# One-core recommender kernel: own-result waits between W1's low parts, a group of gathers moved to the copied table, and new orders for the first two tiles

## The chip, the cores and the metric

The kernel runs on one core of one Trainium2 chip. The metric is the device time of one execution in microseconds (us); three runs of the kernel before took 774.78, 777.32 and 778.52, the median is 777.32.

The core's engines run programs of their own and meet in semaphores: TensorE (PE) multiplies and transposes, VectorE (DVE) and ScalarE (ACT) do elementwise steps, GpSimd (POOL) issues the gathers, SyncE (SP) the plain DMAs.

## The reference

A batch of 2048 rows is scored. Each row has 13 continuous values and 26 categories. Every category picks a row of 64 numbers in a table of 12500 rows; every continuous value scales one of the table's first 13 rows. The 39 vectors, their 741 pairwise dot products and two dense layers with layer norm give one number a row:

```python
cont_emb = emb_table[:CONT_FIELD][None, :, :] * conts[:, :, None]
cate_emb = emb_table[cates]
cc = jnp.concatenate([cont_emb, cate_emb], axis=1)
gram = jnp.einsum('bfd,bgd->bfg', cc, cc)
pairs = gram[:, ROWS, COLS]
X = jnp.concatenate([cont_emb.reshape(B, -1), cate_emb.reshape(B, -1), pairs], axis=1)
X = jax.nn.relu(_layernorm(X @ W1 + b1, ln1_g, ln1_b))     # W1: 3237 x 1024
X = jax.nn.relu(_layernorm(X @ W2 + b2, ln2_g, ln2_b))     # W2: 1024 x 1024
logit = jax.nn.sigmoid(X @ Wout + bout)
```

Categories may lie past the table's end; such an index means the last row.

## The kernel before

**Tiles.** The batch is cut into 16 tiles of 128 rows. For a tile, the 26 fields' rows are gathered into `xb`, one gather of 128 rows for each field, in four groups: fields 0-7, 8-13, 14-19, 20-25 (`GROUPS` counts pairs of fields). TensorE transposes a group (L570, "own 1" to "own 3" and "next 0"), then 19 k-tiles of 128 rows of W1 are multiplied into the sums: 0 to 12 are gathered rows, 13 to 18 are features (pairs, continuous values). Between them stand the gram products (L612), whose results ScalarE and VectorE take out of PSUM (`take_dots`), turn into features and hand back to TensorE for transposing ("factor", "late").

**Split numbers.** Every operand is used as a rounded high part and the rest, its low part, so a k-tile is six matmuls (high times high, high times low, low times high, in two halves of 512 columns; L546 to L548). For W1 this is done once: ScalarE rounds part k (`w1_hi_part`, L855), VectorE subtracts that from the raw part (`w1_lo_part`, L1129, a tensor_tensor of 128x1024 with both inputs in SBUF). For each transposed group ScalarE rounds (`split_group`, L787), VectorE subtracts (L1115), and both make copies for the gram products (`gram_copies`, L794 and L800; `still_low`, L1123).

**Order.** Nothing is scheduled by a program at run time: each engine runs its list in the order written. TensorE's order in a tile is a tuple: `FIRST` for tile 0, `SECOND` for tile 1, `STEADY` for the others. A number is a k-tile (13 and up belong to the tile before, except at the end), "own g" a group's transposes, "v n" products of the continuous rows of W1. ScalarE and VectorE have their counterparts in `first_tile`, `second_tile` and `iteration`.

**Gathers.** GpSimd (`gather`, L494) issues 26 gathers a tile in the order of the fields, from L510 or L513. There is one `xb`, so a group's gathers of tile x+1 wait until that group of tile x is transposed (`trans_ready`). In the loop further waits (`progress`) tie them loosely to TensorE's other steps. The table lies in DRAM as it came; indices past its end can't be gathered from it, so tile 0's gathers check bounds and skip such rows (L510), and ScalarE has filled `xb` with the last row before (`fill`, L867). Meanwhile SyncE copies the table into a scratch table with 128 copies of the last row behind it (four copies, `table_in`, and `last_rows_in`); the index of an absent row is set to one of these (`limit`), and from tile 1 on the gathers need no check (L513). The copies stand in SyncE's list of loads behind W1's part 6; each load waits until the one four places ahead has landed (L438).

**Start.** VectorE first makes tile 0's indices (`index_chain`), then the others, then the constants of the gram products, then `cont_features(0)`, and then W1's low parts 0 to 3.

## Time and profile before

| | |
|---|---|
| median of 3 runs | 777.32 us |
| the profiled execution | 778.39 us, its span 776.9 us |
| mean granted TensorE clock | 0.979 of full |
| busy: PE, DVE, ACT, POOL | 731.6, 582.2, 516.1, 481.3 us |
| gathers from the copied table | 390, 978 ns each |

The span is what the trace covers; about 1.5 us of the time lie outside it. Busy time leaves out the issue of DMAs and waits on semaphores. In a timeline a row gives the start, the duration, the engine, the line, what is written from what, and in brackets how long the engine idled before and what it waited for; "x4" merges four instructions in a row. "<-issue" is a gap in which the engine waited for nothing that the profile shows; between two gathers of GpSimd it is 0.30 us. A landing is the time from a DMA's issue to its end; for a gather the issue is the start of its row.

### The profile page before, as it was taken

Reading aid. Unit: us, or ns where it says so; the run is one execution under the profiler, and the core shown is the slowest. Engines: PE = TensorE matmul, PEld = TensorE weight load, DVE = VectorE, ACT = ScalarE, POOL = GpSimd, SP = SyncE. Lnnn points to the kernel's source line nnn. Section 1 sums busy time; section 2 is a strip of 40 time slices with the busy share of each in tenths; the row PEclk is TensorE's granted clock in tenths of the full one; section 3 lists DMA queues with packets and bytes.
Section 4 is the critical chain, followed back from the end, with each engine's and each line's share of the span. In section 5 each row is a group of like instructions: output and inputs, shape, how many; then the busy total and the mean of one; then the engine's idle time right before and its main releaser. Section 6 shows DMA issues by size and latency. Waiting matters only on the chain.

```text
span 776.9 us, 11960 instructions
## 1 busy us (share of the span) xinstructions
PE 731.6 (94%) x3583; PEld 596.8 (77%) x3583; DVE 582.2 (75%) x1735; ACT 516.1 (66%) x978; POOL 481.3 (62%) x450
## 2 busy tenths in 40 slices
PE   5598899999999999999999999999999999999995
PEld 1356778888888888778788877878878888888884
DVE  7357977878878888787787877878787566565568
ACT  3487877868778687686867868677665535545441
POOL 6777877777777777777777777777000433434431
PEclk9798979999999999999999999999999999999998
DMA  8961111111111111111111111112463111101000
GB/s 323 347 228 25 23 54 28 54 54 26 54 39 40 52 25 52 34 45 52 25 54 25 52 54 26 52 25 59 176 216 124 55 29 54 54 27 54 27 1 0
DMA packets 26644, 53.37 MB, mean 69 GB/s; under 512 B 11024, under 2 KB 11351, under 8 KB 26554
## 3 DMA queue, kind: packets, MB, share of 16 engines
q1 hardware_dynamic: 10570, 31.29, 12.0%
q0 software_dynamic: 13312, 13.06, 7.3%
q10 hardware_dynamic: 2736, 8.71, 2.8%
q8 instruction: 12, 0.20, 0.1%
q14 instruction: 14, 0.11, 0.1%
HBM read 45.20 MB, written 11.63 MB: 73 GB/s over the span
## 4 chain that ended last, share of the span: by engine, by line
PE 44%; POOL 30%; issue 17%; DVE 4%; DMA 2%; ACT 2%; POOLq 0%; ACTq 0%; DVEq 0%
POOL xb L513 27%; PE acc L546 13%; PE acc L548 13%; PE acc L547 13%; POOL xb L510 3%; PE gr L612 1%; PE tr L612 1%; DMA xb<-in_L_rec_emb_table,idx_all 1%; PE gr L714 1%; PE tr L714 1%; DMA xb<-table_scratch,idx_all 1%; PE tr L570 0%; PE gr L570 0%; DMA last_row<-in_L_rec_emb_table 0%; ACT dots L830 0%
## 5 line engine op out<-in xcount | busy, mean ns | idle before, releaser
L513 POOL DMA_INDIRECT xb<-table_scratch,idx_all x390 | 381.3, 978 | 118.9 <-issue 116.4
L546 PE MATMUL acc<-w_hi,x_hl 128*128 128x512 f32 x416 | 172.9, 416 | 4.5 <-DVE x_hl L1115 3.1
L548 PE MATMUL acc<-w_hi,x_hl 128*128 128x512 f32 x416 | 165.5, 398 | 0.0
L547 PE MATMUL acc<-w_lo,x_hl 128*128 128x512 f32 x416 | 165.0, 397 | 0.0
L530 POOL TENSOR_TENSOR raw_lo<-raw_lo,raw_hi 128x1024 f32<-128x1024 f32 x14 | 33.5, 2391 | 146.8 <-ACT raw_lo L998 146.8
L546 PE MATMUL acc<-w_hi 128*128 128x512 f32 x256 | 100.9, 394 | 0.0
L548 PE MATMUL acc<-w_hi,w_lo 128*128 128x512 f32 x256 | 99.7, 389 | 0.0
L547 PE MATMUL acc<-w_lo,w_hi 128*128 128x512 f32 x256 | 99.7, 389 | 0.0
L794 ACT CAST g_still<-x_hl 64x384 fp32r<-64x384 f32 (+1 forms) x128 | 97.9, 765 | 2.5
L546 PEld LDWEIGHTS acc<-w_hi,x_hl 128*128 128x128 f32 x416 | 80.0, 192 | 20.8 <-issue 4.1
L548 PEld LDWEIGHTS acc<-w_hi,x_hl 128*128 128x128 f32 x416 | 79.7, 192 | 18.5
L547 PEld LDWEIGHTS acc<-w_lo,x_hl 128*128 128x128 f32 x416 | 80.2, 193 | 13.3
L546 PE MATMUL acc<-w_hi,f_slots 128*128 128x512 f32 x192 | 77.9, 406 | 1.5 <-DVE w_lo L1129 1.5
L548 PE MATMUL acc<-w_hi,f_slots 128*128 128x512 f32 x192 | 75.0, 391 | 0.0
L547 PE MATMUL acc<-w_lo,f_slots 128*128 128x512 f32 x192 | 75.0, 390 | 0.0
L1369 DVE TENSOR_TENSOR w_lo<-raw_lo,w_hi 128x256 fp32r<-128x256 f32 x64 | 34.9, 564 | 50.4 <-ACT w_hi L990 50.3
L800 ACT ACTIVATE g_move<-x_hl 64x384 fp32r<-64x384 f32 (+1 forms) x128 | 70.3, 549 | 1.5
L800 ACT CAST g_move<-x_hl 64x384 fp32r<-64x384 f32 (+1 forms) x128 | 69.0, 539 | 1.9
L836 ACT ACTIVATE st<-st 128x1 f32<-128x1 f32 x32 | 6.5, 203 | 77.6 <-DVE st L1219 77.6
L548 PEld LDWEIGHTS acc<-w_hi,w_lo 128*128 128x128 f32 x256 | 48.1, 188 | 10.0
L547 PEld LDWEIGHTS acc<-w_lo,w_hi 128*128 128x128 f32 x256 | 48.1, 188 | 9.4
L546 PEld LDWEIGHTS acc<-w_hi 128*128 128x128 f32 x256 | 48.1, 188 | 9.5
(121 smaller groups left out, 1313.3 us busy)
## 6 DMA issues: line engine op xcount, KB each, us to landing
raw_lo<-in_L_rec_W SPq DMA_DIRECT2D x26, 512.0 KB, 5.4
h_scratch<-h_row ACTq DMA_DIRECT2D x16, 512.0 KB, 2.9
raw_hi<-h_scratch SPq DMA_DIRECT2D x16, 512.0 KB, 3.5
xb<-table_scratch,idx_all POOLq DMA_INDIRECT x390, 2.4
table_scratch<-in_L_rec_emb_table SPq DMA_DIRECT2D x4, 781.2 KB, 7.9
raw_hi<-in_L_rec_W SPq DMA_DIRECT2D x6, 512.0 KB, 5.7
raw_hi<-in_L_rec_b SPq DMA_DIRECT2D x1, 512.0 KB, 4.3
raw_hi<-in_L_rec_ln_g SPq DMA_DIRECT2D x1, 512.0 KB, 5.2
```

The costliest lines, as they stand in the source:

```text
L510: done = nc.gpsimd.indirect_dma_start(out=to, out_offset=None, in_=emb, in_offset=at_row, bounds_check=VOCAB - 1, oob_is_err=False)
L513: done = nc.gpsimd.indirect_dma_start(out=to, out_offset=None, in_=table, in_offset=at_row)
L530: nc.gpsimd.tensor_tensor(a2[par][:, :], n2[par][:, :], g2_bc, ALU.mult).then_inc(a2_mul, 1)
L546: nc.tensor.matmul(o, a, w, start=first, stop=False)
L547: nc.tensor.matmul(o, a, v, start=False, stop=False)
L548: return nc.tensor.matmul(o, b, w, start=False, stop=last)
L612: last = nc.tensor.matmul(to, g_still[:, SAMPLES * j:SAMPLES * (j + 1), :].rearrange("p s f -> p (s f)"), g_move[:, :, j:P:P // SAMPLES], ...
L714: last = nc.tensor.transpose(t[:, k // 4, (k % 4) * P:(k % 4 + 1) * P], h1[par][:, k * P:(k + 1) * P], ident[:, :])
L794: nc.scalar.copy(still_to(0, a, b, of), still_from(a, b, of))
L800: last = nc.scalar.mul(to, x_hi, 2.0) if m % 2 else nc.scalar.copy(to, x_hi)
L836: nc.scalar.activation(st[:, 1:2], st[:, 0:1], ACT.Sqrt).then_inc(sqrt_done, 1)
L1369: TT(y_lo[:, par, part, :], y[:, part, :], y_hi[:, par, part, :].bitcast(F32), ALU.subtract).then_inc(y_split, 1)
```

## The change

It has five parts.

1. `w1_lo_part(k)` waits, for k of 1 and more, until part k-1 is reported done (`w1_split`), so VectorE waits for its own result.
2. Tile 0's fourth group (fields 20 to 25) is gathered from the copied table without a check. The waits for the four copies and the last rows move from behind tile 0's gathers to ahead of these six, with one for all indices; that group isn't filled, and the first index chain makes 20 columns instead of 26.
3. SyncE issues the first load of `e13` ahead of `last_row`.
4. W1's parts stand elsewhere. Before: 0-3, 4, 5-6, 7, 8, 9-10, 11, 12, then 13 to 18 one by one. After, on VectorE: 0-5, 6, 7-8, 9-12, 13-14, 15-16, 17-18, and `cont_features(0)` behind part 6. ScalarE rounds in the same groups up to 12, and 13 to 18 in one go as before.
5. In tiles 0 and 1 the order is new: in `FIRST` the v products stand one place earlier each, in `SECOND` "late prev" comes after k-tiles 13, 14 and 4; `copy_v` goes ahead of the first `take_dots`; in tile 1 `take_dots(1, 0)` goes into `norm1(0)`, behind the root.

```diff
-FIRST = (0, 1, 2, 3, "own 1", 4, 5, 6, "own 2", "v 3", 7, 8, "v 4", "own 3", "v 5", 9, 10, "gram 0", "gram 1", 11,
+FIRST = (0, 1, 2, 3, "own 1", 4, 5, 6, "v 3", "own 2", "v 4", 7, 8, "v 5", "own 3", 9, 10, "gram 0", "gram 1", 11,
          "gram 2", "gram 3", "next 0", 12)
-SECOND = (0, 1, 2, 3, "factor prev", "own 1", "late prev", 13, 4, 14, 5, 15, 6, "own 2", 16, 17, 18, 7, "own 3", 8, 9,
+SECOND = (0, 1, 2, 3, "factor prev", "own 1", 13, 14, 4, "late prev", 15, 5, 6, "own 2", 16, 17, 18, 7, "own 3", 8, 9,
           "gram 0", "gram 1", 10, "gram 2", "gram 3", 11, "next 0", 12)
...
+            sp.dma_start(e13[:, 0, :], emb[0:CONT, :]).then_inc(e13_in, 16)
             sp.dma_start(last_row[:, :], emb[VOCAB - 1:VOCAB, :].to_broadcast([P, DIM])).then_inc(last_row_in, 16)
-            sp.dma_start(e13[:, 0, :], emb[0:CONT, :]).then_inc(e13_in, 16)
...
                 for g, (a, b) in enumerate(GROUPS):
-                    if first:
+                    bounded = first and g < NG - 1
+                    if bounded:
                         pool.wait_ge(filled, g + 1)
+                    elif first:
+                        pool.wait_ge(idx_done, 2)
+                        table_whole()
...
-            for g in range(NG):
+            for g in range(NG - 1):
                 fill(g)
-            w1_hi_parts(0, 1, 2, 3)
+            w1_hi_parts(0, 1, 2, 3, 4, 5)
             split_group(0, 0)
-            w1_hi_part(4)
+            w1_hi_part(6)
             act.wait_ge(setup_done, 1)
             gram_copies(0, 0)
-            w1_hi_parts(5, 6)
             split_group(0, 1)
             gram_copies(0, 1)
-            w1_hi_part(7)
+            w1_hi_parts(7, 8)
...
                 split_group(0, 2)
-                w1_hi_part(8)
                 gram_copies(0, 2)
-                w1_hi_parts(9, 10)
+                w1_hi_parts(9, 10, 11, 12)
                 split_group(0, 3)
                 gram_copies(0, 3)
-                w1_hi_part(11)
+                copy_v()
                 for q in range(FILLS):
                     take_dots(0, q, first=True)
-                w1_hi_part(12)
-                copy_v()
...
                 dve.wait_ge(w1_rounded, k + 1)
+                if k >= 1:
+                    dve.wait_ge(w1_split, k)
                 TT(w1_lo[:, k, :], raw_lo[k][:, :], w1_hi[:, k, :].bitcast(F32),
                    ALU.subtract).then_inc(w1_split, 1)
...
+            w1_lo_parts(0, 1, 2, 3, 4, 5)
+            split_group(0, 0)
+            w1_lo_part(6)
+            still_low(0, 0)
             cont_features(0, first=True)
-            w1_lo_parts(0, 1, 2, 3)
-            split_group(0, 0)
-            w1_lo_part(4)
-            still_low(0, 0)
-            w1_lo_parts(5, 6)
             split_group(0, 1)
             still_low(0, 1)
-            w1_lo_part(7)
+            w1_lo_parts(7, 8)
```

## Rows read from the trace of the kernel before

**Rows 1.** The page: chain that ended last, shares of span by line.

```profile
POOL xb L513 27%; PE acc L546 13%; PE acc L548 13%; PE acc L547 13%; POOL xb L510 3%; PE gr L612 1%; PE tr L612 1%; DMA xb<-in_L_rec_emb_table,idx_all 1%; PE gr L714 1%; PE tr L714 1%; DMA xb<-table_scratch,idx_all 1%; PE tr L570 0%; PE gr L570 0%; DMA last_row<-in_L_rec_emb_table 0%; ACT dots L830 0%
```

**Rows 2.** TensorE's waits, total, times, longest; 110-300 us, then 300-580.

```profile
PE acc L546 <- DVE x_hl L1115: 0.3, 1, 0.3
...
PE gr L570 <- DMA xb<-table_scratch,idx_all: 7.1, 8, 1.1
```

**Rows 3.** Transposes of group 0, tiles 2 and 3; GpSimd's timeline, 117 us.

```profile
L570 PE MATMUL tr<-ident,xb x4: 290/404/421, 109.3 to 109.9; 128*128 128x128 f32 x4
...
L570 PE MATMUL tr<-ident,xb x4: 270/272/273, 141.3 to 141.7; 128*128 128x128 f32 x4
...
117.69 0.94 POOL L513 DMA_INDIRECT xb<-table_scratch,idx_all  x1 [0.30 <-issue]
```

**Rows 4.** GpSimd's groups in three stretches: busy, mean ns | idle before.

```profile
L510 POOL DMA_INDIRECT xb<-in_L_rec_emb_table,idx_all x26 | 32.2, 1239 | 12.4 <-issue 7.6 <-ACT xb L867 4.8
...
L513 POOL DMA_INDIRECT xb<-table_scratch,idx_all x32 | 36.4, 1138 | 9.8 <-issue 9.4 <-PE tr L570 0.3
...
L513 POOL DMA_INDIRECT xb<-table_scratch,idx_all x359 | 345.9, 963 | 109.4 <-issue 107.3 <-PE tr L570 0.9 <-PE tr L612 0.6
```

**Rows 5.** TensorE's timeline: start us, us, instruction, [idle before].

```profile
549.37 0.55 PE L570 MATMUL gr<-ident,xb 128*128 128x128 f32 x3 [0.78 <-DMA xb<-table_scratch,idx_all]
```

**Rows 6.** GpSimd's timeline: gathers of tiles 0 and 1.

```profile
6.24 1.34 POOL L510 DMA_INDIRECT xb<-in_L_rec_emb_table,idx_all  x1 [4.75 <-ACT xb L867]
...
14.39 1.00 POOL L510 DMA_INDIRECT xb<-in_L_rec_emb_table,idx_all  x1 [0.30 <-issue]
15.69 5.53 POOL L510 DMA_INDIRECT xb<-in_L_rec_emb_table,idx_all  x1 [0.30 <-issue]
...
37.48 1.54 POOL L510 DMA_INDIRECT xb<-in_L_rec_emb_table,idx_all  x1 [0.30 <-issue]
...
51.20 1.55 POOL L513 DMA_INDIRECT xb<-table_scratch,idx_all  x1 [0.30 <-issue]
53.06 0.94 POOL L513 DMA_INDIRECT xb<-table_scratch,idx_all  x1 [0.30 <-issue]
```

**Rows 7.** VectorE's timeline: setup's end, low parts 0-3, parts 9-10.

```profile
12.86 0.70 DVE L1108 MEMSET g_still<- 64x768 f32 x1 [0.20 <-issue]
...
15.73 4.63 DVE L1129 TENSOR_TENSOR w_lo<-raw_lo,w_hi 128x1024 fp32r<-128x1024 f32 x4
...
50.71 2.36 DVE L1129 TENSOR_TENSOR w_lo<-raw_lo,w_hi 128x1024 fp32r<-128x1024 f32 x2 [1.92 <-ACT w_hi L855]
```

**Rows 8.** VectorE's timeline: the second step waits for the first.

```profile
5.57 0.36 DVE L1054 TENSOR_SCALAR spare<-spare 128x390 f32<-128x390 f32 x1
5.96 0.57 DVE L1056 TENSOR_TENSOR spare<-spare 128x390 f32<-128x390 f32 x1
```

**Rows 9.** ScalarE's timeline: W1's third rounded half.

```profile
14.97 1.04 ACT L855 CAST w_hi<-raw_lo 128x1024 fp32r<-128x1024 f32 x1 [0.38 <-DMA raw_lo<-in_L_rec_W]
```

**Rows 10.** SyncE's timeline: the load that waits for the last table copy.

```profile
30.07 0.33 SPq L438 DMA_DIRECT2D raw_hi<-in_L_rec_W  x1
```

**Rows 11.** DMA issues at 14.39, 15.69, 46.36 us: issue to landing.

```profile
xb<-in_L_rec_emb_table,idx_all POOLq DMA_INDIRECT x1, 6.0
...
xb<-in_L_rec_emb_table,idx_all POOLq DMA_INDIRECT x1, 12.7
...
xb<-table_scratch,idx_all POOLq DMA_INDIRECT x1, 5.9
```

**Rows 12.** TensorE's timeline: three starts after a wait.

```profile
28.49 1.09 PE L570 MATMUL tr<-ident,xb 128*128 128x128 f32 x4 [7.32 <-DMA xb<-in_L_rec_emb_table,idx_all]
...
66.69 0.79 PE L546 MATMUL acc<-w_hi,x_hl 128*128 128x512 f32 x1 [1.36 <-DVE w_lo L1129]
...
79.11 0.50 PE L546 MATMUL acc<-w_hi,f_slots 128*128 128x512 f32 x1 [1.54 <-DVE w_lo L1129]
```

**Rows 13.** Busy PE, PEld, DVE, ACT, POOL; granted clock, DMA share, GB/s.

```profile
97.00:110.00 13.00, 11.41 (x49) 9.62 (x49) 9.78 (x24) 8.60 (x17) 9.68 (x11) 0.61 0.21 66
```

More of the change, by code:

```diff
@@ L492, in progress, with table_whole @@
                     stands_alone(pool)
+            def table_whole():
+                for n in range(COPIES):
+                    pool.wait_ge(table_in[n], 16)
+                pool.wait_ge(last_rows_in, 16)
             def gather(x, par, first=False, tied=False):
@@ L508, in gather @@
                         at_row = bass.IndirectOffsetOnAxis(ap=idx[:, par, f:f + 1], axis=0)
-                        if first:
+                        if bounded:
                             done = nc.gpsimd.indirect_dma_start(out=to, out_offset=None, in_=emb, in_offset=at_row,
@@ L516, in _ @@
             gather(0, 0, first=True)
-            for n in range(COPIES):
-                pool.wait_ge(table_in[n], 16)
-            pool.wait_ge(last_rows_in, 16)
             gather(1, 1)
@@ L918, in first_tile @@
                 split_group(1, 1)
+                still_copies(1, 0)
+                move_copies(1, 0, (0, 1))
                 late_features_hi(0)
-                still_copies(1, 0)
+                move_copies(1, 0, (2, 3))
                 tail_features_hi(0)
-                move_copies(1, 0)
             def second_tile():
@@ L930, in second_tile @@
                 gram_copies(1, 3)
-                norm1(0, 0)
+                root(0)
+                take_dots(1, 0)
+                norm1(0, 0, rooted=True)
                 h1_store(0)
-                for q in range(FILLS):
+                for q in range(1, FILLS):
                     take_dots(1, q)
@@ L1058, in index_chain @@
                 TS(to.bitcast(I32), f, 0.0, most, ALU.max, ALU.min).then_inc(count, 1)
-            index_chain(0, 0, CATE, idx[:, 0, :], float(VOCAB), idx_done)
+            bounded = 2 * GROUPS[NG - 1][0]
+            index_chain(0, 0, bounded, idx[:, 0, 0:bounded], float(VOCAB), idx_done)
             dve.wait_ge(rows_in, 16)
             nc.vector.tensor_copy(limit[:, :], rows_sb[:, :]).then_inc(idx_step, 1)
-            index_chain(4, CATE, TILES * CATE, idx_all[:, CATE:TILES * CATE], limit[:, 0:1])
+            index_chain(4, bounded, TILES * CATE, idx_all[:, bounded:TILES * CATE], limit[:, 0:1])
             dve.wait_ge(idx_step, 8)
@@ L1285, in first_tile @@
                 split_group(0, 2)
-                w1_lo_part(8)
                 still_low(0, 2)
-                w1_lo_parts(9, 10)
+                w1_lo_parts(9, 10, 11, 12)
                 split_group(0, 3)
@@ L1291, in first_tile @@
                 indices(2, 0)
-                w1_lo_part(11)
                 for q in range(FILLS):
                     take_dots(0, q, first=True)
-                w1_lo_part(12)
                 split_group(1, 0)
@@ L1298, in first_tile @@
                 cate_features(0)
+                w1_lo_parts(13, 14)
+                factor_lo(0)
+                split_group(1, 1)
                 cate_pairs(0)
-                factor_lo(0)
-                w1_lo_part(13)
-                split_group(1, 1)
+                w1_lo_parts(15, 16)
                 late_features_lo(0)
-                w1_lo_part(14)
                 tail_features_lo(0)
-                w1_lo_part(15)
                 still_low(1, 0)
-                w1_lo_part(16)
             def second_tile():
+                w1_lo_parts(17, 18)
+                split_group(1, 2)
                 still_low(1, 1)
-                w1_lo_part(17)
-                split_group(1, 2)
-                w1_lo_part(18)
                 still_low(1, 2)
@@ L1320, in second_tile @@
                 indices(3, 1)
-                norm1(0, 0)
-                for q in range(FILLS):
+                norm1(0, 0, lambda: take_dots(1, 0))
+                for q in range(1, FILLS):
                     take_dots(1, q)
```

## The prediction

> **What bounds the kernel now.** I read the chain that ended last first [rows 1]: the largest single entry is GpSimd issuing the gathers of the tile loop, 27% of the span in busy time and most of the 17% "issue" beside it, and no TensorE line has more than 13%. So although TensorE is busy 94% of the span, the end of the tile loop hangs on another engine. The waits of TensorE show when [rows 2]: between 110 and 300 us it waits 0.3 us in all, between 300 and 580 us it waits 7.1 us in eight pieces, each for the rows that a gather brings. The pace explains it. TensorE starts tile 2 at 109.3 and tile 3 at 141.3, 32.0 us a tile [rows 3]. GpSimd makes 359 gathers from 92 us to the last in 345.9 + 109.4 us [rows 4], which is 1.268 us each and 26 x 1.268 = 33.0 us a tile. TensorE begins late, gains about 1 us a tile on GpSimd, catches up at about 300 us and from there goes at GpSimd's pace. The last gathered group is transposed at 549.37 after a wait of 0.78 us for its DMA [rows 5], and the rest follows from it. Hence the rule for this change: **the end moves by what GpSimd's last gather moves**, as long as TensorE's work on the first tiles doesn't fall back by more than those 7.1 us against it.
>
> GpSimd in turn never waits in the loop for TensorE: every gap between gathers is its usual 0.30. When tile 3's first gather starts at 117.69, the transposes that free its buffer are long done (they start at 109.3) [rows 3]; the margin is some 7.6 us. So what matters on GpSimd is how long each gather takes. Undisturbed, one takes 1.00 us against the input table and 0.94 against the copied one [rows 6]. In tile 0 the 26 take 1239 ns on average, from 46 to 92 us 32 take 1138 ns, and after that 963 [rows 4]. The excess is 26 x 0.24 = 6.2 and 32 x 0.194 = 6.2, together **12.4 us**, all of it in the time in which VectorE makes W1's low parts.
>
> Rows 6 and 7 together show what holds GpSimd. The gather at 15.69 takes 5.53 us and ends at 21.22; VectorE's four low parts run back to back from 15.73 to 20.36, and the gather ends 0.86 after them. The gather at 51.20 ends at 52.75; a low part runs from 50.71 to 51.93, and again it ends 0.82 later, in the middle of the next low part. So a gather needs something 0.13 us into its run that a low part holds for its 1.22 us; having got it, it needs 0.82 to 0.87 more. In the second case the following part had only just got its rounded half from ScalarE, and the gather came in between; in the first all were ready ahead, and it didn't until all four were over. All but two of the longer gathers up to 92 us end like this behind a low part (the two are the first, 0.34 us too long [rows 6], and one with some 0.15), so of the 12.4 us about 11.9 belong to the 19 low parts: 4.5 to the first four and 7.4 to the other fifteen, 0.49 each.
>
> **The change, part by part.**
>
> *The wait between low parts.* VectorE may begin part k only when part k-1 is reported done. Steps that wait for their own engine's result follow at 0.04 us behind the end (5.57 + 0.36, then 5.96) [rows 8], where unhindered parts overlap by 0.08 (four take 4.63, not 4.88) [rows 7]: 0.12 us for each part that follows another directly, 12 of them, 1.4 us of VectorE spread over 75 us. In the first train the loads set the pace anyway (next edit), so the idle time covers it there; it isn't covered ahead of split_group(0, 3), which waits behind parts 9 to 12 (four waits, 0.5 us; below). What it brings: between two parts what the gather needs is free for about 0.04 us, so a waiting gather should hold out one part at most. After it got in, it asks again 1.30 us later (0.87 + 0.30 + 0.13; 1.25 against the copied table), and the parts recur every 1.26: they nearly keep step, so a train of parts costs one wait at its start, not one for each part. The pair at 50.71 behaves so already: the first part holds a gather for 0.61, the second none (53.06 takes 0.94) [rows 6, 7]. What the trace can't show is a train of four or six ready parts with the wait; its bounds are 0 and the full back-to-back time.
>
> *The order of the low parts.* Now they come as 0-5, 6, 7-8, 9-12, 13-14, 15-16, 17-18: seven trains. Taking cont_features(0) from ahead of part 0 lets VectorE begin at 13.6 instead of 15.73 [rows 7]. The parts then come at the pace of the loads, 1.4 us (a rounded half takes 1.04 and waits 0.38 for its DMA) [rows 9], with gaps of 0.15 to 0.2, so the first train is loose. I take 0.55 for each of the seven (near the 0.49 of the isolated ones), and 0.8 more for what gets out of step inside the trains of six and four: 7 x 0.55 + 0.8 = 4.6, plus the 0.5 of the two others, 5.1. Gain on GpSimd 12.4 - 5.1 = **7.3 us**; bounds 2.4 (every part still costs 0.5) and about 10 (nothing but the looseness is left), and below nothing if the gap doesn't let the gather in (a rival below).
>
> [...]
>
> *Group 3 of tile 0 from the copied table.* Six gathers at 1.25 instead of 1.30 apart: 0.3 us gained. The new waits stand ahead of them on GpSimd, where the whole loop's gathers queue behind. The copies' last piece has landed when SP issues the load at 30.07, which waits for it [rows 10]. Before, the group's first gather starts at 37.48 [rows 6]; it comes at about 34 to 35 now. So 4 us of cover, and each us beyond would cost one us at the end. These gathers now bring whole rows, 32 KB each, while W1 still loads; the first such gather in that traffic lands 5.9 us after its issue, 2.0 of them its making, no later than those from the input [rows 11]. Their indices now come from the second chain of steps, whose third step begins at 5.96 [rows 8]. The last fill disappears from ScalarE (0.5 us, off every path).
>
> *The first rows swapped on SP.* last_row lands some 0.45 us later, and the first fill with it; the first gather waits for its indices too, and starts 0.9 after those. I charge 0.2 us, bounds 0 and 0.45.
>
> *TensorE, VectorE and ScalarE in tiles 0 and 1.* Here only TensorE's place relative to GpSimd is at stake. Group 0 lands at 28.4, 12.7 us after the issue of its last gather, where the one before took 6.0 [rows 11]; with the gather ending at 17 to 18 it lands at 22 to 24, and TensorE's 7.32 us wait [rows 12] shrinks by 5. A little is lost at split_group(0, 3), behind parts 9 to 12 (it ends at about 51 now, at 53.7 before). Part 12's wait for its low half (66.69, 1.36 us) goes, of that at 79.11 (1.54) half, since parts 13 to 16 stand earlier; and gram 2 of tile 1 no longer sits behind all of norm1 on ScalarE; before, the granted clock there is 0.61 over 13 us [rows 13], part of them at the lower of the two levels. "late prev" moves back by three k-tiles, some 4 us; the gather of tile 2's field 10 waits for it, but is due only after 36 gathers from 46 us on, past 90 us, where "late prev" comes near 75. Together TensorE comes into tile 2 by 8 to 11 us earlier, so more than GpSimd. It then catches GpSimd some three tiles sooner, and there two things follow: its waits grow from 7.1 to about 10 us, and GpSimd goes in locked step with the loop, where gathers lose 0.6 us a tile to short VectorE steps instead of the 0.15 to 0.3 of the free tiles (average 0.47: 0.018 x 26). I charge 1.0 for that, bounds 0 and 1.5.
>
> **The sum:** 7.3 + 0.3 - 0.2 - 1.0 = 6.4 us. The profiled run took 778.39 (span 776.9), 1.1 over the median of the runs; 778.4 - 6.4 = 772.0 for a like run and 777.3 - 6.4 = 770.9 for the median. I say **771**.
>
> **The rivals.**
> (a) *Every low part still costs its 0.5 us*, trains or not, because gathers and parts don't fall into step. Then 19 x 0.5 + 0.5 = 10 us of excess stay, gain 2.4 + 0.3 - 0.2 = 2.5: 774.8. For it: the trains of one and two have shown nothing longer. Against it: the pair at 50.71.
> (b) *The wait opens nothing* (slower). A gap of 0.04 us is too short, and the gather that asks at a train's start comes in at its end. Then the train 0-5 holds from 14.5 to about 22.3, 7.8 us, 9-12 4.4, four pairs 1.8 each (7-8, 13-14, 15-16, 17-18), part 6 0.55: 20 us against 12.4, so 8 slower with the small terms: 785. It decides once the holds exceed 12.4, that is when more than about ten parts pass in closed trains. For it: the 5.53 at 15.69. Against it: no part there waited for anything, and in the pair the gather got in without any gap.
> (c) *The trains cost nothing* and TensorE's head start isn't spent: gain about 10, 767.
> [...]
>
> **How the numbers follow.** The forecast 0.66 (its own range 767.5 to 774), (a) 0.15, (b) 0.08, (c) 0.08, (d) 0.03. The range 766 to 777 takes in the forecast, (a) and most of (c). A measurement of this kernel can tell about 0.5% from no change, 3.9 us: faster is below 773.4. Faster: most of the forecast and (c), 0.70; same: (a), (d) and the forecast's upper edge, 0.23; slower: 0.07.
>
> **What would show it.** No gather over about 2.3 us; mean gather of tile 0 near 1.10 us instead of 1.24, and near 1.03 from there to the last low part; last gather starting near 539 instead of 545.3; TensorE waiting for gathered rows from about 200 us on, in more pieces; tile 2 starting near 100. It would be wrong if the gather of field 20 starts late behind the table, if a gather still spans several low parts, or if TensorE's waits in the loop vanish, since then TensorE and not GpSimd sets the end.

## The result and the profile after

| | before | after |
|---|---|---|
| median of 11 runs | 777.32 us (774.13 to 778.52) | 770.82 us (769.32 to 774.43) |
| the profiled execution, its span | 778.39, 776.9 | 770.79, 769.3 |
| ratio of the runs | | 0.9928, 95% interval 0.9911 to 0.9945 |

The changed kernel is faster by 0.7%, 6.5 us in the medians, 5.6 us by the ratio and 7.6 us between the two profiled executions. The forecast was 771, from a gain of 6.4 us.

The line of the page that answers to [rows 1], the chain that ended last, still has the gathers of the loop first (L513 has become L523, the transposes' L570 L577, the low parts' L1129 L1138):

```profile
POOL xb L523 26%; PE acc L553 14%; PE acc L554 13%; PE acc L555 13%; PE gr L619 1%; PE tr L619 1%; PE gr L721 1%; PE tr L721 1%; DMA xb<-in_L_rec_emb_table,idx_all 1%; PE tr L577 1%; ACT g_move L807 1%; DMA h_scratch<-h_row 1%; DVE w_lo L1138 1%; DVE g_still L1130 1%; DVE dots L1204 1%
```

GpSimd's timeline of the changed kernel: the stretch of the 5.53 us gather of [rows 6], the first gather from the copied table, the longest gather of the kernel, and the last:

```profile
13.01 1.00 POOL L520 DMA_INDIRECT xb<-in_L_rec_emb_table,idx_all  x1 [0.30 <-issue]
14.31 1.29 POOL L520 DMA_INDIRECT xb<-in_L_rec_emb_table,idx_all  x1 [0.30 <-issue]
15.91 1.02 POOL L520 DMA_INDIRECT xb<-in_L_rec_emb_table,idx_all  x1 [0.30 <-issue]
17.24 1.02 POOL L520 DMA_INDIRECT xb<-in_L_rec_emb_table,idx_all  x1 [0.31 <-issue]
...
33.91 0.96 POOL L523 DMA_INDIRECT xb<-table_scratch,idx_all  x1 [0.30 <-issue]
...
37.68 1.99 POOL L523 DMA_INDIRECT xb<-table_scratch,idx_all  x1 [0.30 <-issue]
...
538.12 0.95 POOL L523 DMA_INDIRECT xb<-table_scratch,idx_all  x1 [0.30 <-issue]
```

VectorE's timeline beside it: the first six low parts and the four of the later train.

```profile
13.51 7.87 DVE L1138 TENSOR_TENSOR w_lo<-raw_lo,w_hi 128x1024 fp32r<-128x1024 f32 x6
...
45.49 5.21 DVE L1138 TENSOR_TENSOR w_lo<-raw_lo,w_hi 128x1024 fp32r<-128x1024 f32 x4 [2.71 <-ACT w_hi L862]
```

The first low part (13.51 to 14.73) holds the gather at 14.31 until its end, which costs 0.29; from then on the gathers come between the parts and lose 0.02 each. The last gather starts at 538.12, where it started at 545.31 before: 7.2 us earlier. The groups of GpSimd's gathers up to 60 us answer to [rows 4] (mean ns of one):

```profile
L520 POOL DMA_INDIRECT xb<-in_L_rec_emb_table,idx_all x20 | 21.5, 1075 | 10.6 <-issue 5.5 <-ACT xb L874 4.8 <-DMA table_scratch<-in_L_rec_emb_table 0.3
L523 POOL DMA_INDIRECT xb<-table_scratch,idx_all x20 | 20.6, 1028 | 6.1 <-issue 6.1
```

Below, "excess" is the sum over a kernel's gathers of what each takes beyond 1.00 us (input table) or 0.945 us (copied table), added up from the timeline. Up to 92 us it is 12.4 us before and 5.0 after; from 92 us on 6.1 and 6.3. A gather "asks" about 0.12 us into it: the 0.94 that an undisturbed one takes less the 0.82 that it still takes once let in (0.13 of the 1.00 against the input table, with 0.87); what it does at that point isn't shown. Of the 5.0 us the first parts of the seven trains hold back gathers by 0.29, 0.95, 1.05, 0.29, 0, 0.94 and 0.52 us, 0.58 on average.

TensorE's waits from 300 to 580 us answer to [rows 2], its first transposes of tile 2 to [rows 3]:

```profile
PE gr L577 <- DMA xb<-table_scratch,idx_all: 6.6, 8, 1.0
...
L577 PE MATMUL tr<-ident,xb x4: 272/272/273, 101.1 to 101.4; 128*128 128x128 f32 x4
```

Tile 2 starts at 101.1 instead of 109.3. TensorE's granted clock at tile 1's end, 0.61 in [rows 13] (0.50 in every us from 100 to 109, 1.00 in the three before 99 and from 110 to 111), is 0.88 in the 10 us up to its end now, and 0.95 in the next 10 us (busy time by stretch: PE, PEld, DVE, ACT, POOL, granted clock, DMA share, GB/s):

```profile
90.00:100.00 10.00, 7.16 (x42) 6.45 (x43) 8.55 (x22) 7.97 (x16) 7.56 (x9) 0.88 0.24 79
100.00:110.00 10.00, 9.55 (x45) 7.36 (x43) 9.60 (x42) 8.42 (x13) 7.87 (x8) 0.95 0.11 28
```

One table carries much of what follows (e8_after is the changed kernel profiled once more). It is read from the timelines: excess up to 92 us and behind it, start of tile 2 on TensorE, length of a tile in the early and the late loop, last gather, start of the last gathered group's transposes, and the time of the same execution.

| kernel | excess to 92, after | tile 2 | a tile, early and late | last gather | last transposes | time |
|---|---|---|---|---|---|---|
| before | 12.4, 6.1 | 109.3 | 32.0, 33.1 | 545.3 | 549.4 | 778.4 |
| after | 5.0, 6.3 | 101.1 | 32.0, 33.1 | 538.1 | 541.7 | 770.8 |
| e1_before_wait | 8.6, 4.5 | 104.9 | 32.0, 33.1 | 540.1 | 543.6 | 772.7 |
| e2_after_nowait | 6.9, 6.1 | 101.9 | 32.0, 33.1 | 539.8 | 543.2 | 772.2 |
| e3_after_notable | 4.1, 5.4 | 101.9 | 32.0, 33.1 | 536.4 | 540.0 | 769.0 |
| e4_before_cont | 5.8, 7.0 | 102.5 | 32.0, 33.1 | 539.8 | 543.3 | 775.1 |
| e5_tensor_more | 5.6, 5.9 | 102.4 | 32.0, 33.1 | 537.7 | 541.2 | 770.2 |
| e6_gpsimd_more | 6.1, 6.6 | 100.3 | 32.8, 33.1 | 543.8 | 547.4 | 776.4 |
| e8_after | 6.7, 7.2 | 102.4 | 32.0, 33.2 | 540.3 | 543.8 | 774.8 |
| e9_halves | 4.9, 5.9 | 107.1 | 32.0, 32.7 | 537.4 | 540.9 | 770.8 |
| e11_pairs4 | 6.3, 0.0 | 104.6 | 32.4, 32.4 | 532.8 | 541.2 | 770.9 |
| e12_pairs2 | 4.6, -0.6 | 103.1 | 33.2, 33.2 | 534.1 | 551.3 | 781.3 |

### The profile page after: what moved, and what is told of

Its sections match the earlier page's. It is cut to its first block, busy times and chain, and to the rows that moved or that the text cites. A ratio compares the mean times of both kernels' runs of the same rounds, so it can differ in the third digit from the quotient of the medians.

```text
span 769.3 us, 11972 instructions
## 1 busy us (share of the span) xinstructions
PE 727.8 (95%) x3583; PEld 593.4 (77%) x3583; DVE 582.9 (76%) x1735; ACT 515.9 (67%) x977; POOL 474.0 (62%) x450
## 4 chain that ended last, share of the span: by engine, by line
PE 47%; POOL 27%; issue 15%; DVE 6%; DMA 2%; ACT 2%; POOLq 0%; SPq 0%; ACTq 0%; DVEq 0%
POOL xb L523 26%; PE acc L553 14%; PE acc L554 13%; PE acc L555 13%; PE gr L619 1%; PE tr L619 1%; PE gr L721 1%; PE tr L721 1%; DMA xb<-in_L_rec_emb_table,idx_all 1%; PE tr L577 1%; ACT g_move L807 1%; DMA h_scratch<-h_row 1%; DVE w_lo L1138 1%; DVE g_still L1130 1%; DVE dots L1204 1%
## 5 line engine op out<-in xcount | busy, mean ns | idle before, releaser
L523 POOL DMA_INDIRECT xb<-table_scratch,idx_all x396 | 384.8, 972 | 120.7 <-issue 120.1
```

The source lines that it names most:

```text
L523: done = nc.gpsimd.indirect_dma_start(out=to, out_offset=None, in_=table, in_offset=at_row)
```

## The experiments

### Is the wait worth something by itself?

e1_before_wait: the kernel before with the wait alone.

```diff
                 dve.wait_ge(w1_rounded, k + 1)
+                if k >= 1:
+                    dve.wait_ge(w1_split, k)
```

> The kernel before with the own-result wait alone. Theory (the wait opens the train): the gather at 15.69 us gets in after the first low part, at 16.95, and ends 0.87 later, so it takes about 2.1 us instead of 5.53; the next ones keep step and lose about 0.1 each. Gain on GpSimd 3.2 us, the median about 774 against 777.3. The other low parts stand alone or in pairs that were already open: nothing more. Rival (the wait opens nothing, a gap that short is too short): the gather still takes 5.5 us or a little more, 777.3. Rival (TensorE sets the end, not GpSimd): the gather gets short but the time stays at 777.3.

Measured: 772.82 us median, ratio 0.9954 (0.9936 to 0.9972). GpSimd's and VectorE's timelines:

```profile
15.69 2.13 POOL L510 DMA_INDIRECT xb<-in_L_rec_emb_table,idx_all  x1 [0.30 <-issue]
```

```profile
15.73 5.20 DVE L1131 TENSOR_TENSOR w_lo<-raw_lo,w_hi 128x1024 fp32r<-128x1024 f32 x4
```

The gather that starts at 15.69 beside the same four parts takes 2.13 instead of 5.53, as the theory had it (2.1), and the time falls by 3.6 us, over half of what the whole change brings (the kernel before, run beside it on the same chip, has a median of 776.37). "The wait opens nothing" has fallen.

e2_after_nowait: the changed kernel with those two lines taken out again.

> The changed kernel without the own-result wait. Theory: the first six parts are paced by the loads (1.4 us apart) and stay open even so, no gather above 1.3 us there; but parts 9 to 12 and the pairs 13-14, 15-16, 17-18 have their rounded halves ready ahead, close up, and hold a gather until the train's end: up to 4.6 us at 46 us and up to 2.3 us at each pair. GpSimd loses some 3.5 us against the changed kernel, 774.3 (range 772.5 to 777). Rival (the order alone did it, the wait gives nothing): 770.8 with the same gathers as in the changed kernel. Rival (b) of the forecast turned round (the waits only cost VectorE its 0.19 us a part): 770 or less.

Measured: 773.61 us median, ratio 0.9977 (0.9958 to 0.9996). So without the wait a third of the gain is left by the ratios, and the wait is worth 2.8 us in the medians, 3.8 by the ratios, on top of the new order. The one profiled execution says less: it took 772.18 us, its excess is 6.9 against 5.0 and its last gather starts 1.6 us later than the changed kernel's; four of the twelve runs took 776.5 to 777.9, and none of those was profiled. Nor do the traces show the loss where I had put it. GpSimd and VectorE around the train 9 to 12, around 13 and 14, and around 15 and 16:

```profile
47.55 1.33 POOL L523 DMA_INDIRECT xb<-table_scratch,idx_all  x1 [0.30 <-issue]
49.18 1.96 POOL L523 DMA_INDIRECT xb<-table_scratch,idx_all  x1 [0.30 <-issue]
...
67.69 0.94 POOL L523 DMA_INDIRECT xb<-table_scratch,idx_all  x1 [0.30 <-issue]
...
74.20 3.01 POOL L523 DMA_INDIRECT xb<-table_scratch,idx_all  x1 [0.30 <-issue]
```

```profile
46.84 4.63 DVE L1136 TENSOR_TENSOR w_lo<-raw_lo,w_hi 128x1024 fp32r<-128x1024 f32 x4 [2.71 <-ACT w_hi L862]
...
66.58 2.37 DVE L1136 TENSOR_TENSOR w_lo<-raw_lo,w_hi 128x1024 fp32r<-128x1024 f32 x2
...
71.71 2.42 DVE L1210 TENSOR_TENSOR dots<-h_row 128x25 f32<-128x25 f32 x25
74.05 2.35 DVE L1136 TENSOR_TENSOR w_lo<-raw_lo,w_hi 128x1024 fp32r<-128x1024 f32 x2
```

The train 9 to 12 runs back to back (4.63 us for four) and lets a gather in twice: the one at 47.55 ends at 48.88, the one at 49.18 at 51.14, each 0.82 behind the end of one part. It is open. The pair at 74.05 isn't: its gather ends at 77.21, 0.81 behind both parts. What differs is what VectorE did before: it idled 2.71 us ahead of the first, and came without a gap from 25 short steps into the second. The four parts of the kernel before [rows 7] came without a gap from cont_features' twelve short steps:

```profile
14.10 1.72 DVE L1144 SCALAR_TENSOR_TENSOR feats<-ee_bc,c 128x12 f32<-128x12 f32 x12
```

The pair at 66.58 came without a gap from seven short steps, and the gather at 67.69, which asked just as its first part ended, wasn't held. Whether seven are too few or the moment was lucky isn't shown. Within the first train, where I expected no gather above 1.3 us, one that starts at 15.97 takes 2.04.

e4_before_cont: the kernel before with cont_features(0) moved and nothing else.

```diff
-            cont_features(0, first=True)
             w1_lo_parts(0, 1, 2, 3)
             split_group(0, 0)
             w1_lo_part(4)
             still_low(0, 0)
+            cont_features(0, first=True)
```

> The kernel before with one move only: cont_features(0) goes from ahead of W1's low parts 0 to 3 to behind still_low(0, 0). No wait is added. Theory: the parts begin at 13.6 us and then follow the rounded halves, 1.4 us apart, so none is ready ahead: the train is open by itself and the 5.53 us gather becomes one of at most 2.2. Gain 4 us on GpSimd, 773.3 - the same as the wait gives, from the other side. Rival (only a reported result opens the train): a gather of 4 us or more remains between 14 and 21 us, 777.

Measured: 773.34 us median, ratio 0.9960 (0.9942 to 0.9978). GpSimd's timeline of e4_before_cont has no gather above 1.9 us:

```profile
14.37 1.86 POOL L510 DMA_INDIRECT xb<-in_L_rec_emb_table,idx_all  x1 [0.30 <-issue]
16.54 1.30 POOL L510 DMA_INDIRECT xb<-in_L_rec_emb_table,idx_all  x1 [0.30 <-issue]
```

So the wait and the move each take the 5.53 us gather away by themselves. Added to the kernel before, they bring 3.6 and 3.0 us in the medians (776.37 beside them on the same chip), 3.6 and 3.1 by the ratios. e4 can't tell why the move helps: its parts no longer follow short steps, but the second and third also wait 0.38 and 0.35 us for their rounded halves, which is what I had expected, and either can be what lets a gather in. Its excess falls by 6.6 us, more than the time does.

### What holds a gather

Two kernels of their own put gathers beside steps of VectorE of one kind at a time.

```python
# e7_port: for each kind, four steps beside eight gathers (five of the eight kinds; waits between the steps left out here)
TT(r[k][:, :], a[:, :], b[:, :], ALU.subtract)             # two inputs in SBUF
TT(r[k][:, :], flat(ps), b[:, :], ALU.subtract)            # one in PSUM
TT(flat(pw), a[:, :], b[:, :], ALU.subtract)               # two in SBUF, result in PSUM
nc.vector.tensor_copy(c[:, :], a[:, :])
nc.vector.tensor_scalar(r[k][:, :], a[:, :], 0.5, None, ALU.mult)
```

> A kernel of its own that computes nothing of the reference; its output is a constant. GpSimd issues 64 gathers of 128 rows back to back, then 24 plain DMAs of 128 rows; during every eight of them VectorE runs one train of four steps of 128x1024 and then idles: (1) tensor_tensor with both inputs in SBUF, (2) the same with an own-result wait, (3) one input in PSUM, (4) copies f32 SBUF to SBUF, (5) both inputs in SBUF and the result in PSUM with own-result waits, (6) tensor_scalar SBUF to SBUF, (7) tensor_tensor with a short copy between, (8) the same in halves of 512; beside the plain DMAs (1), (4) and nothing. [...]

VectorE's timeline of e7_port, and GpSimd's beside it:

```profile
7.75 4.63 DVE L92 TENSOR_TENSOR r<-a,b 128x1024 fp32r<-128x1024 f32 x4 [1.40 <-issue]
...
28.00 4.62 DVE L97 TENSOR_TENSOR r<-ps,b 128x1024 fp32r<-128x1024 f32 x4 [10.20 <-POOLq L55]
...
54.12 5.08 DVE L104 TENSOR_TENSOR pw<-a,b 128x1024 f32<-128x1024 f32 x4 [10.60 <-POOLq L55]
67.05 2.62 DVE L106 TENSOR_SCALAR r<-a 128x1024 fp32r<-128x1024 f32 x4 [7.85 <-POOLq L55]
...
106.59 4.63 DVE L92 TENSOR_TENSOR r<-a,b 128x1024 fp32r<-128x1024 f32 x4 [8.43 <-POOLq L55]
```

```profile
8.72 1.10 POOL L61 DMA_INDIRECT xb<-in_emb,idx  x1 [0.30 <-issue]
10.12 1.94 POOL L61 DMA_INDIRECT xb<-in_emb,idx  x1 [0.30 <-issue]
...
28.92 0.94 POOL L61 DMA_INDIRECT xb<-in_emb,idx  x1 [0.30 <-issue]
30.16 0.95 POOL L61 DMA_INDIRECT xb<-in_emb,idx  x1 [0.30 <-issue]
...
54.24 1.92 POOL L61 DMA_INDIRECT xb<-in_emb,idx  x1 [0.89 <-DMA xb<-in_emb,idx]
...
67.23 1.33 POOL L61 DMA_INDIRECT xb<-in_emb,idx  x1 [0.61 <-DMA xb<-in_emb,idx]
...
108.29 0.53 POOL L63 DMA_DIRECT2D xb<-in_emb  x1 [1.17 <-DMA xb<-in_emb,idx]
110.00 0.53 POOL L63 DMA_DIRECT2D xb<-in_emb  x1 [1.18 <-DMA xb<-in_emb,idx]
```

The trace has 64 gathers, 0.30 us apart beside the first three kinds and up to 1.10 later, and 24 plain DMAs. VectorE idles 0.42 us between the first two trains and 6.29 to 10.63 ahead of each other one. What the gathers that asked during each train took:

| VectorE's steps of 128x1024 | gathers in order, us |
|---|---|
| tensor_tensor, both inputs in SBUF | 1.10, 1.94 |
| the same, own-result waits | 1.22, 0.96, 0.95, 0.95 |
| tensor_tensor, one input in PSUM | 0.94, 0.95, 0.94 |
| copies f32, SBUF to SBUF | 1.33, 0.94 |
| both inputs in SBUF, result in PSUM, own-result waits | 1.92, 0.97, 0.94 |
| tensor_scalar, SBUF to SBUF | 1.33, 1.19 |
| both inputs in SBUF, a short copy between | 1.88, 0.94, 0.94 |
| both inputs in SBUF, in halves of 512 | 1.33, 0.94, 1.01 |

Beside steps with one input in PSUM a gather takes its 0.94 to 0.95. Beside steps with two inputs in SBUF it is held even when their result goes to PSUM (54.24: 1.92, ending 0.82 behind the first step), and also by tensor_scalar and by copies (1.33 each, 0.82 behind a step's end), until the end of the one step that runs; the second gather beside the copies (0.94) asked just as one of them ended (42.89). Plain DMAs issued by GpSimd take 0.53 to 0.55 beside the same tensor_tensor train that holds gathers, and 0.53 beside nothing. So for tensor_tensor what counted is where VectorE reads and not where it writes, and a plain DMA wasn't held by it. Why a gather is held and a plain DMA isn't, the rows don't show. Where an own-result wait or a short copy stands between the steps, one gather takes 1.22 or 1.88 us and the next 0.94 to 0.96.

Copies are another case: beside them plain DMAs take up to 0.84 us, and four in a row end 0.11 to 0.12 us behind the end of a copy each (the first at 118.32, behind 118.20). They are held too, so which side a copy holds isn't separated here, and tensor_scalar wasn't run beside plain DMAs.

But no gather as long as the 5.53 us of [rows 6] came: four ready parts back to back (from 7.75) let a gather in behind the first and behind the third (it ends at 9.82 and 12.06), where the kernel before had them closed. The halves were open too, with 1.33 us at most. The second kernel asks what makes the difference.

> A kernel of its own that computes nothing of the reference; its output is a constant. GpSimd issues gathers of 128 rows back to back. Beside them VectorE runs trains of tensor_tensor steps of 128x1024 with both inputs in SBUF, each kind three times at three offsets of some 0.3 us: (1) four after idling, (2) four directly behind 12 short scalar_tensor_tensor steps with two SBUF inputs, (3) four behind 25 short tensor_tensor steps, (4) four behind 12 short copies, (5) as (2) with an own-result wait before all but the first of the four, (6) eight after idling, (7) four after idling, each with a wait that is met long ahead. Question: in the kernel before four parts held one gather to their end, but four in the last kernel of this sort let one in at every end. [...] Theory B (waits that are met ahead make the difference): (7) closed, (2) to (4) as (1). Theory C (it's the moment at which the gather asks): no kind is always closed, and it depends on the offset alone.

The gathers beside each train of four (each kind three times; "eight" is one train of eight steps):

| VectorE before the four parts | longest gather in the three tries, us |
|---|---|
| 12 short scalar_tensor_tensor steps | 4.78, 5.02, 5.31 |
| 25 short tensor_tensor steps | 5.12, 5.37, 4.39 |
| 12 short copies | 5.22, 5.46, 4.46 |
| 12 short steps, own-result waits between the four | 1.35, 1.61, 1.90 |
| idle (two of three tries ran into each other) | 1.97 |
| idle, eight parts | 1.97, 1.98, 1.97 |
| idle, each part with a wait met long ahead | 1.97, 1.98, 1.96 |

Nine of nine trains behind short steps are closed: the gather ends 0.82 behind the last part. One of them, VectorE and then GpSimd:

```profile
71.76 1.86 DVE L101 SCALAR_TENSOR_TENSOR shorts<-a,b,c 128x12 f32<-128x12 f32 x12 [10.45 <-ACTq L79]
73.54 4.62 DVE L114 TENSOR_TENSOR r<-a,b 128x1024 fp32r<-128x1024 f32 x4
```

```profile
73.67 5.31 POOL L65 DMA_INDIRECT xb<-in_emb,idx  x1 [0.30 <-issue]
```

All the others are open (1.98 us at most). It made no difference whether the short steps were tensor_tensor (4.39 to 5.37), scalar_tensor_tensor (4.78 to 5.31) or copies (4.46 to 5.46), nor whether the parts carry a wait that is met long ahead (1.96 to 1.98; theory B), nor which of the three moments it was (theory C); in all nine the gather asked while the first part ran. With the own-result wait the train behind short steps was open three times of three (1.35 to 1.90). Why a run of short steps closes what follows isn't shown; the rows show only that it did.

The rows of this kernel show a second use of the wait, in GpSimd's timeline beside a train of four with it (from 202.34) and a train of eight without it (from 242.81):

```profile
202.75 1.61 POOL L65 DMA_INDIRECT xb<-in_emb,idx  x1 [0.30 <-issue]
204.67 0.96 POOL L65 DMA_INDIRECT xb<-in_emb,idx  x1 [0.30 <-issue]
205.93 0.95 POOL L65 DMA_INDIRECT xb<-in_emb,idx  x1 [0.31 <-issue]
...
243.71 1.15 POOL L65 DMA_INDIRECT xb<-in_emb,idx  x1 [0.30 <-issue]
245.16 1.97 POOL L65 DMA_INDIRECT xb<-in_emb,idx  x1 [0.30 <-issue]
247.43 1.97 POOL L65 DMA_INDIRECT xb<-in_emb,idx  x1 [0.30 <-issue]
249.70 1.98 POOL L65 DMA_INDIRECT xb<-in_emb,idx  x1 [0.30 <-issue]
```

Without the wait the parts recur every 1.14 us, a gather asks every 1.25, and so it falls just behind the start of a part again and again: 1.02 us lost each time, in every second part. With the wait they recur every 1.26 and the gathers fit between them: one hold at the start, then 0.01 each. So an open train without waits still cost a third of its length (0.21 and three times 1.02 in 9.17 us); one with waits cost one hold (0.67 us here).

### Does GpSimd set the end?

e5_tensor_more gives TensorE work, e6_gpsimd_more gives GpSimd work, both early in the kernel.

```diff
# e5_tensor_more
-                for kt in range(a, b):
+                again = 12 if isinstance(x, int) and x == 2 and g == 2 else 1
+                for kt in [kt for _ in range(again) for kt in range(a, b)]:
# e6_gpsimd_more
             gather(0, 0, first=True)
+            for n in range(26):
+                if n >= 1:
+                    pool.wait_ge(idled, n)
+                nc.gpsimd.memset(small[:, 15:16], 0.0).then_inc(idled, 1)
             gather(1, 1)
```

> The changed kernel; in tile 2 TensorE makes the transposes of group 2 twelve times instead of once, the same values into the same place: 33 transposes of 0.11 us, 3.7 us more of TensorE's work, just past the start. Theory (GpSimd sets the end of the tile loop, TensorE has 7.6 us of waits to give): TensorE's waits for gathered rows shrink from 7.6 to about 4 us and the time stays within 1 us of 770.8. Rival (TensorE sets the end): the time rises by 3.7 us to 774.5 and the waits stay.

> The changed kernel; between tile 0's and tile 1's gathers GpSimd makes 26 small memsets of one unused column, each waiting for the one before. The trace will tell how much that delays the next gather; I estimate 4 us from the 0.45 us pitch of GpSimd's two dependent steps at the start less their size, so anything from 3 to 12. Theory (GpSimd sets the end): the time rises by what the last gather is late, one for one, within 1 us. Rival (TensorE sets the end and GpSimd is ahead): less than half of it arrives.

Measured: 769.74 us for e5 (0.9906, 0.9877 to 0.9936) and 776.27 us for e6 (0.9989, 0.9973 to 1.0004). TensorE's waits from 105 to 580 us, first of e5, then of e6:

```profile
PE gr L578 <- DMA xb<-table_scratch,idx_all: 3.3, 4, 1.0
```

```profile
PE gr L582 <- DMA xb<-table_scratch,idx_all: 12.7, 14, 1.9
```

In e5 tile 2 takes 35.2 us instead of 31.7, TensorE's waits for gathered rows fall from 7.5 (6.6 from 300 us on, 1.0 before; rounded) to 3.3, and the end doesn't move. In e6 the memsets hold tile 1's first gather back by about 4.5 us and the excess is 1.1 higher; the last gather comes 5.7 later, the profiled time is 5.6 longer, and TensorE waits 5.2 us more. One for one, as predicted. The column of last gathers says the same: in all kernels of the table but e4, e8, e11 and e12 the time is 232.4 to 233.4 us behind it. In e4 it is 235.3: there TensorE waits once for VectorE's features behind the last gather, 2.4 us where the changed kernel waits 1.3, and its granted clock in the stretch from 560 to 570 us is 0.83 against 1.00. In e8 it is 234.4, with 3.1 us of that wait. So the end is the last gather's to within some 2 us, which are lost behind it. TensorE's own start counts for little: in e9 it comes into tile 2 at 107.1, 6 us later than in the changed kernel, and the time is the same.

### Can more be had there?

e8_after is the changed kernel again, on the chip of the next one.

> The changed kernel itself, on the same chip as the next one. All theories: 770.8, 0.9928 of the kernel before; GpSimd's excess over undisturbed gathers in the first 90 us again about 5 us, in other places by how the low parts fall.

> The changed kernel with every low part made in two steps of 512 columns, each waiting for the one before. Theory (a gather is held by the one step that runs when it asks for its indices, and gets in at that step's end): a hold costs at most 0.69 us instead of 1.22, the seven trains cost 0.3 each instead of 0.55 on average, and the excess goes from 5.2 to about 3 us; but steps now recur every 0.78 us and no longer keep step with the gathers (1.30), so inside the trains a gather may meet a step each time at a new place: up to 0.3 each. Time 769 to 771. Rival (each such wait costs VectorE 0.19 us and that counts, or the holds are as many as steps): 771 to 773, or excess unchanged.

```diff
-                TT(w1_lo[:, k, :], raw_lo[k][:, :], w1_hi[:, k, :].bitcast(F32),
-                   ALU.subtract).then_inc(w1_split, 1)
+                for h in range(2):
+                    if 2 * k + h:
+                        dve.wait_ge(w1_split, 2 * k + h)
+                    part = slice(h * HALF, (h + 1) * HALF)
+                    TT(w1_lo[:, k, part], raw_lo[k][:, part], w1_hi[:, k, part].bitcast(F32),
+                       ALU.subtract).then_inc(w1_split, 1)
```

Measured: 771.00 for e8 (0.9927, 0.9905 to 0.9949), 770.70 for e9 (0.9922, 0.9901 to 0.9944): the same. In e8's own profiled execution (774.76 us) the excess was 6.7, in e9's (770.76) 4.9: most single holds are shorter (0.2 to 0.3; two take 0.5 and 0.6), but 18 gathers lose over 0.12 us where 8 did, since steps every 0.76 us don't fit a gather. The theory's doubt about the step was right and its 3 us weren't; that a gather asks for its indices at that moment was my guess, and the rows show only that it is held there. e8 against the first profile of the same kernel also tells how much one execution differs from the next: the excess up to 92 us by 1.7 us, the last gather by 2.2, the time by 4.0, of which 1.8 are lost behind the last gather.

e11_pairs4 and e12_pairs2 put own-result waits into the 25 short steps of cate_pairs, in which most later tiles hold a gather for 0.5 us.

```diff
                 for f in range(CATE - 1):
+                    if f and f % 4 == 0:                       # e12: every second
+                        dve.wait_ge(pair_step, 6 * x + f // 4)
                     last = TT(chosen[:, cate_at(f):cate_at(f + 1)], S[:, f, f + 1:CATE], S[:, f + 1:CATE, f], ALU.add)
+                    if (f + 1) % 4 == 0:
+                        last.then_inc(pair_step, 1)
```

> The changed kernel, and VectorE also waits for its own result after every fourth of the 25 short steps that add up a tile's category pairs. In the changed kernel a gather is held about 0.5 us in this run of steps in ten of the fourteen later tiles. Theory (what a gather needs isn't handed over inside a run of short steps, and GpSimd still sets the end): a wait every 0.4 us lets it in, the holds of 0.5 become 0.2 at most, GpSimd saves 2 to 4 us over the loop, VectorE spends 0.6 us more a tile in time it has; 768 (767 to 770). Rival (the hold has another cause, or TensorE takes over as the bound since VectorE is later): excess in the loop stays at 6 us or TensorE waits for VectorE instead; 771 or more.

> The same with a wait after every second step. Theory: the holds there fall to 0.1, but VectorE spends 1.2 us more a tile; 768 if VectorE has that time, otherwise above the kernel with a wait after every fourth, and TensorE's or ScalarE's waits for VectorE show it.

Measured: 770.87 (0.9922, 0.9893 to 0.9952) and 782.55 (1.0075, 1.0047 to 1.0103). The holds of the loop vanish in e11: excess 0.0 instead of 6.3, last gather at 532.77, 5.4 us earlier than in the changed kernel. Nothing of it arrives in the time. TensorE's waits from 105 to 580 us, first of e11, then of e12:

```profile
PE tr L592 <- DVE feats L1178: 1.6, 1, 1.6
PE acc L554 <- DVE x_hl L1123: 1.4, 2, 1.2
```

```profile
PE acc L554 <- DVE x_hl L1123: 13.3, 14, 1.6
```

TensorE no longer waits for a gather at all, and a tile takes 32.4 us from the first to the last, where it took 32.0 while TensorE was free and 33.1 while GpSimd led. The six waits a tile cost TensorE's own loop 0.4 us in each of 13 tiles, some 5 us; with twelve waits a tile takes 33.2, and TensorE waits for VectorE's low half of a group in every tile. The bound changed hands. That e11 comes out even is partly chance: TensorE came into tile 2 at 104.6, 3.5 us later than in the changed kernel. That delay was there at tile 1's first transposes (63.57 against 60.05), ahead of the first of the edited steps; the granted clock from 50 to 60 us was 0.66 against 1.00. With the changed kernel's start TensorE would have ended the loop some 3.5 us sooner, by my estimate from these rows; the six runs' median (770.87) doesn't show such a gain.

### The fourth group's table

> The changed kernel with tile 0's fourth group again gathered from the input with bounds check, filled before, and the waits for the copies behind it. Theory: six gathers 0.05 us further apart, 0.3 us on GpSimd, so 771.1 against 770.8, within what can be told. Rival (the copied table landed the group earlier for TensorE and that counted): TensorE's own 3 moves by over 1 us and the time by over 2.

The edit puts `bounded = first` back, with tile 0's fourth fill, its 26 columns of indices, and the table's waits behind tile 0's gathers. Measured: 771.87 us median, ratio 0.9954 (0.9938 to 0.9969) against 0.9928 (0.9911 to 0.9945) of the changed kernel; yet the profiled execution is the quickest of all, with the last gather at 536.4. The medians differ by 1.0, the ratios by 2.0 us, the forecast was 0.3, and the intervals overlap: it can't be told whether this part gives anything.

## Why the prediction was right

**The bound.** Right. The last gather moved 7.2 us, the profiled time 7.6, and e5 and e6 show both sides of it. TensorE catches up with GpSimd at 261 us (a tile goes from 31.9 to 33.1 us there), before at 301 us, so one tile sooner and not three; I had said 200, and 10 us of waits, where there are 7.5. That comes from tile 2's start: 8.2 us earlier, the low end of my 8 to 11, and GpSimd itself is 7.6 earlier by then.

**The low parts' 7.3 us.** The size is right: the excess fell from 12.4 to 5.0, and a train cost 0.58 on average for my 0.55; in e8, the same kernel, 1.7 us more excess stayed. The reason I gave for the 5.53 us gather is wrong. I wrote that the train was closed because all its rounded halves were ready ahead. Trains with everything ready were open in e2 and e7 (gathers of at most 1.96 and 1.94 us); closed was what followed a run of 12 or more short steps without a gap (4.39 us and more in e10, 3.01 in e2 at 74 us). In the kernel before that was cont_features(0), so its move alone did away with the long gather (e4), as the wait alone did (e1). I had described that move as a way to begin earlier and to let the loads space the parts; that it also parts the train from the short steps I hadn't seen. In the changed kernel the loads don't space them: the first six parts recur every 1.33 us with the same 0.10 between them as later ones, which is the wait's doing, where I had 1.4 and gaps of 0.15 to 0.2 from the loads. The keeping in step was right (the gathers between the parts of the first train take 1.02 and 1.03) and is what the wait gives to open trains too. My example for it didn't show it: the gather at 53.06 [rows 6] asked only when the pair from 50.71 [rows 7] had ended. My rivals (a), (b), (c) and (d) all fall: of the 5.0 us at most 4.7 belong to the 19 parts, 0.25 each and not 0.5 (a); the longest gather takes 1.99 (b); the trains did cost something (c); and that gathers end 0.82 us behind low parts is no chance (e1, e7, e10), nor is the gain 0.1 us (d).

**The wait's cost.** Mis-sized, without consequence. I took 0.12 us for each of 12 from two short steps that wait for one another [rows 8]. The four parts take 5.21 instead of 4.63, so it is 0.19 each, 2.3 us in all: the part waits for ScalarE's half and its own result, two waits, and the gap is 0.10. In e10, where it waits for its own result alone, it is the 0.12. split_group(0, 3) ends at 51.3, as I had it (51).

**The copied table.** The cover held: the load behind the last copy starts at 29.41, the first of these gathers at 33.91, in time by 4.5 us (I had 4). Its 0.3 us can't be seen.

**The swap on SyncE.** The first gather starts at 6.32 instead of 6.24: 0.1 for my 0.2, and less than its difference between executions (6.10 in e8, the same kernel), so it can't be told either.

**TensorE's start.** Group 0 is transposed at 22.78 after a wait of 1.10 instead of at 28.49 after 7.32 (I had 22 to 24). It counts for the balance alone.

**The loop's 1.0 us.** Mis-sized. The gather that starts at 92.54 in the kernel before starts at 84.99, 7.6 us ahead, and the last one is 7.2 ahead: the loop gave back 0.4, since TensorE catches up one tile sooner and not three.

**The sum.** 7.3 + 0.3 - 0.2 - 1.0 = 6.4 stands against 7.2 of the last gather in one pair of executions (7.4 from the excess, 0.3, -0.1 and -0.4) and 6.5 in the medians. In e8's execution the last gather moved by only 5.0. With 2.2 us between two executions of one kernel, that the median came out at 770.8 for 771 is partly luck.

## What to carry to other kernels

Where GpSimd issues gathers one after another and sets the pace, look in its timeline for gathers longer than the usual (0.94 and 1.00 us here), and on VectorE for what ends 0.8 us before each of them ends. Here a tensor_tensor with both inputs in SBUF (up to 1.98 us for the gather in e7 and e10), a copy or a tensor_scalar from SBUF to SBUF (1.33) held a gather until its end, and a tensor_tensor with one input in PSUM didn't (0.94 to 0.95). Don't let several long steps follow a run of a dozen or more short ones without a gap: in e10 one gather took 4.39 to 5.46 us behind such a run. After an idle moment it was at most 1.98 there, with a wait of VectorE for its own result at most 1.90, and the wait brought steps (every 1.26 us) and gathers (every 1.25) into step. Count what the wait costs each engine that comes behind, since once GpSimd is free the next bound may be close: here a tile took 33.1 us at GpSimd's pace and 32.4 at TensorE's with the waits in.

## What the runs showed of the hardware

- A gather of 128 rows issued by GpSimd was held only near its start: having got in, it needed 0.82 us more (0.87 with bounds check), also while the next step ran (e2: 47.55 to 48.88). Of the kinds tried, a tensor_tensor with both inputs in SBUF (1.92 us even with its result in PSUM), a copy and a tensor_scalar (1.33 us each) held it, and a tensor_tensor with one input in PSUM didn't (0.94 to 0.95; e7). VectorE's steps kept their length meanwhile (four in 4.63 us beside held gathers, in 4.62 beside none held; e7).
- A plain DMA issued by GpSimd took 0.53 to 0.55 us beside such a tensor_tensor and up to 0.84 beside copies (e7).
- After 12 to 25 short steps without a gap, four steps of 1.2 us held a gather that asked during the first to the end of all four in nine of nine tries (4.39 to 5.46 us); after idling, never (at most 1.98; e10). A pair behind seven short steps let one in (0.94; e2).
- A wait of VectorE for its own last result cost 0.12 us between plain steps (1.26 instead of 1.14 from one step's start to the next in e10), 0.19 us (1.33 in the changed kernel) when the step also waited for another engine.
- Two executions of the same kernel differed by 1.7 us in how long gathers were held up to 92 us (5.0 and 6.7), and by 2.2 us in the start of the last gather.
